# A transformer block on one core: gates brought to all partitions by DMA, VectorE's gating work and the weight rounding moved

## The reference, cut to what matters

```
logits = xt @ gate_w.T                        # 8 experts
scores = softmax(logits); top_scores, sel = top_k(scores, 2)
for e in range(8):                            # tokens routed to e, scaled by their gate
    xe = where(routed to e, xt * gate_e, 0)
    out_routed += (silu(xe @ w1[e]) * (xe @ w3[e])) @ w2[e]
out = out_routed + (silu(xt @ w1s) * (xt @ w3s)) @ w2s    # the shared expert
```

## Time and profile before

| | |
|---|---|
| median of 3 runs | 990.48 us (988.3 to 992.23) |
| profiled execution | 989.17 us, span 987.4 us, mean granted TensorE clock 0.973 |
| busy, share of the span | PE 874.8 us (89%), weight load 621.0 (63%), VectorE 732.5 (74%), ScalarE 578.9 (59%), GpSimd 528.6 (54%) |
| DMA | 8.70 MB in all, mean 9 GB/s; 235 GB/s in the first fortieth of the span |

### The profile page before, as it was taken

How to read it: one execution, slowest core, us unless ns; L and a number is a source line. 1 busy time by engine, 2 the same in 40 slices (tenths; PEclk the granted TensorE clock), 3 DMA queues, 4 the chain that set the end, 5 groups by cost and what they waited for, 6 DMA issues and landing times.

```text
span 987.4 us, 22246 instructions
## 1 busy us (share of the span) xinstructions
PE 874.8 (89%) x7264; PEld 621.0 (63%) x7264; DVE 732.5 (74%) x1978; ACT 578.9 (59%) x903; POOL 528.6 (54%) x610
## 2 busy tenths in 40 slices
PE   2799999888999999999788888888878799999998
PEld 0355555545688777788555555555545688888887
DVE  4677777766777777777678898989883577767775
ACT  1478778766444434444488888888875344444443
POOL 4666666663444455554436575757542644454551
PEclk9999999988999999999899999999997899999999
DMA  8000000000000000000000000000000000000000
GB/s 235 1 2 1 0 0 0 0 2 2 1 1 1 1 1 0 0 1 1 1 2 1 1 0 0 0 0 0 1 1 1 1 12 12 12 7 4 11 11 23
DMA packets 14607, 8.70 MB, mean 9 GB/s; under 512 B 1616, under 2 KB 14160, under 8 KB 14544
## 3 DMA queue, kind: packets, MB, share of 16 engines
q1 hardware_dynamic: 12960, 7.28, 2.6%
q10 hardware_dynamic: 1584, 0.62, 0.2%
HBM read 5.80 MB, written 2.10 MB: 8 GB/s over the span
## 4 chain that ended last, share of the span: by engine, by line
PE 21%; issue 13%; DVE 11%; POOL 7%; ACT 2%; DVEq 0%; POOLq 0%; ACTq 0%
DVE s_qs L1088 6%; PE psum L819 5%; PE psum L787 5%; POOL f_xe_lo L1434 3%; POOL f_p L1444 3%; PE psum L1327 2%; PE psum L769 2%; PE psum L1289 1%; DVE f_xe L1471 1%; PE psum L885 1%; PE psum L1291 1%; PE psum L1290 1%; PE psum L874 1%; PE psum L804 1%; ACT f_xe_hi L1403 1%
## 5 line engine op out<-in xcount | busy, mean ns | idle before, releaser
L1403 ACT ACTIVATE f_xe_hi<-f_xe 128x512 fp32r<-128x512 f32 x128 | 80.9, 632 | 204.6 <-DVE f_xe L1471 204.6
L1434 POOL TENSOR_TENSOR f_xe_lo<-f_xe,f_xe_hi 128x512 fp32r<-128x512 f32 x64 | 83.9, 1311 | 184.6 <-ACT f_xe_hi L1403 184.6
L1088 DVE TENSOR_REDUCE s_qs<-psum 128x4 fp32r<-128x1024 f32 x128 | 156.3, 1222 | 35.4 <-PE psum L804 34.6
L1327 PEld LDWEIGHTS psum<-w,f_h 128*128 128x128 f32 x1152 | 147.7, 191 | 8.8
L1327 PE MATMUL psum<-w,f_h 128*128 128x128 f32 x1152 | 153.0, 276 | 0.0
L467 ACT ACTIVATE s_probs<-psum 128x1024 f32<-128x1024 f32 x128 | 125.9, 1023 | 33.1 <-PE psum L354 32.7
L955 ACT ACTIVATE s_probs<-psum 128x1024 f32<-128x1024 f32 x128 | 131.3, 1026 | 19.5 <-PE psum L787 17.8
L1289 PE MATMUL psum<-f_xe_hi,w_hi 128*128 128x512 f32 x288 | 127.0, 441 | 7.6 <-POOL f_xe_lo L1434 7.0
L1487 DVE TENSOR_TENSOR f_h<-psum,f_g 128x512 f32<-128x512 f32 x144 | 99.2, 689 | 44.9 <-ACT f_g L1388 34.6
L1291 PE MATMUL psum<-f_xe_lo,w_hi 128*128 128x512 f32 x288 | 114.1, 396 | 0.0
L1290 PE MATMUL psum<-f_xe_hi,w_lo 128*128 128x512 f32 x288 | 113.5, 394 | 0.0
(11 more groups left out here) (177 smaller groups left out, 1732.6 us busy)
## 6 DMA issues: line engine op xcount, KB each, us to landing
out<-x SPq DMA_DIRECT2D x8, 256.0 KB, 2.3
x<-in_x SPq DMA_DIRECT2D x3, 512.0 KB, 9.6
w<-in_w SPq DMA_DIRECT2D x3, 512.0 KB, 7.5
x<-in_x SPq DMA_DIRECT2D x2, 256.0 KB, 3.9
select_raw<-in_select SPq DMA_DIRECT2D x1, 512.0 KB, 4.8
rope_cos<-in_rope_cos SPq DMA_DIRECT2D x1, 256.0 KB, 3.9
rope_sin<-in_rope_sin SPq DMA_DIRECT2D x1, 256.0 KB, 4.6
wqkv_a<-in_Wqkv_aT ACTq DMA_DIRECT2D x1, 192.0 KB, 3.6
```

The source lines that it names most:

```text
L1088: dve.tensor_reduce(o[:, r:r + 2, 2 * p:2 * p + 2, 24:25].bitcast(F32R), room(km, i).rearrange("p (r j s) -> p r j s", r=2, j=2), AX.X, AL ...
L1327: ins = pe.matmul(Y[k % 2][:, t * P:(t + 1) * P], g.f_h[:, q, t * P:(t + 1) * P], g.w2[:, e, :], start=(e == 0 and t == 0), stop=(e == NE ...
L1434: pool.tensor_tensor(xe_lo[:, ring(e), :], src, xe_hi[:, ring(e), :], ALU.subtract).then_inc(xe_lo_pool.sem, 1)
```

## The change

- The gates go to all partitions by DMA. VectorE multiplies the chosen gates by the reciprocal sum as before, then turns them in 32x32 blocks (`dve.transpose` into `f_sg`). SyncE's queue writes `f_sg` (16 KB, runs of 128 bytes) to a DRAM tensor `gates`, waits until that has landed, and then loads for each expert one row of 512 gates to all 128 partitions (`f_gt`, 256 KB, a ring of four). For the experts after the first four, and from the second chunk on for all, SyncE waits before each load until VectorE has used the buffer. `scale` now multiplies two SBUF tensors. The selecting matmuls, `s_turn`, `f_st`, `f_ss`, the two instructions that filled it, and the selecting matrices with their load and rounding are gone.
- The norm, transposes, logits, choice and powers of a chunk are done two chunks ahead instead of one, in slots 4 to 8; `best` is cut into `best` and `masks`, `gates` into `sums` and `gates`, `residual` into `residual` and `stats`, each in its own slot. The shared expert's rounding moves from its own turn to slot 2.
- `LOW_ON_DVE` goes from four experts to two; GpSimd's `low` goes from five to seven per chunk.
- `LEAD` starts the feed-forward slots one attention slot earlier in most cases. In attention B two waits for bank 5 and for `f_st` go or come earlier.
- Opening: x is loaded in eight parts, those from the third on only after `first_loads` have landed; ScalarE runs one small exponential before its remaining DMA issues; VectorE's wait for `first_loads` moves from before the first norm to step -2; statistics and roots are spread anew; the Newton rounds of the first two sequences run on VectorE.
- w1 and w3 are rounded in slot 11 of steps 12 and 13, their rests are made in slot 5 of steps 13 and 14.
- The output stores of the second feed-forward layer are issued between the gate loads of chunk m and m+2.

The core of the diff; "..." marks what is left out:

```diff
-PARTS = ((0, 4), (4, 8), (8, 16), (16, 24), (24, 32))
-STATISTICS = ((-3, 0), (-2, 11), (-1, 12), (0, 8), (0, 12))
-ROOTS = ((-3, 0), (-2, 15), (-1, 15), (0, 15), (1, 5))
+PARTS = tuple((t, t + 4) for t in range(0, NT, 4))
+LOADED = ((0, 1), (1, 1), (2, 2), (2, 2), (3, 4), (3, 4), (3, 4), (3, 4))
+STATISTICS = {(-3, 0): (0,), (-3, 11): (1, 2), (-2, 3): (3,), (-2, 12): (4, 5), (-1, 12): (6, 7)}
+ROOTS = {(-3, 0): (0,), (-2, 5): (1, 2, 3), (-1, 5): (4, 5), (0, 5): (6, 7)}
...
-            sp.dma_start(g.x[:, lo:hi, :], x_view[:, lo:hi, :]).then_inc(x_loaded[i], 16)
+            if i == 2:
+                sp.wait_ge(first_loaded, first_count)
+            sp.dma_start(g.x[:, lo:hi, :], x_view[:, lo:hi, :]).then_inc(x_loaded[LOADED[i][0]], 16)
...
+                act.wait_ge(filled, 1)
+                act.activation(tiny[:, 60:61], g.minus_half[:, 0:1], ACT.Exp)
...
+            if (k, h) == (-2, 2):
                 dve.wait_ge(first_loaded, first_count)
...
+NEWTON_ON_DVE = 2
...
-            if k in (13, 14):
-                pool.wait_ge(g.late_loaded, g.late_count)
-                pool.wait_ge(w_hi_sb.sem, k - 12)
-                w, hi, lo = ((g.w1, g.w1_hi, g.w1_lo), (g.w3, g.w3_hi, g.w3_lo))[k - 13]
-                pool.tensor_tensor(lo[:], w[:], hi[:], ALU.subtract)
+                if k in (13, 14) and h == 5:
+                    pool.wait_ge(w_hi_sb.sem, k - 12)
+                    w, hi, lo = ((g.w1, g.w1_hi, g.w1_lo), (g.w3, g.w3_hi, g.w3_lo))[k - 13]
+                    pool.tensor_tensor(lo[:], w[:], hi[:], ALU.subtract)
...
+                if km < NEWTON_ON_DVE:
+                    dve.wait_ge(seed.sem, seed.upto(m))
+                    i = 0
+                    for o, u, w, op in newton_steps():
+                        if i:
+                            dve.wait_ge(newton.sem, newton.upto(m, i))
+                        dve.tensor_tensor(o[:], u[:], w[:], op).then_inc(newton.sem, 1)
...
-            if k == 12:
-                dve.wait_ge(g.late_loaded, g.late_count)
-                dve.tensor_copy(g.w1_hi[:], g.w1[:]).then_inc(w_hi_sb.sem, 1)
-                dve.tensor_copy(g.w3_hi[:], g.w3[:]).then_inc(w_hi_sb.sem, 1)
-                dve.tensor_copy(g.select[:], g.select_raw[:])
             for h in part:
+                if k in (12, 13) and h == 11:
+                    dve.wait_ge(g.late_loaded, g.late_count)
+                    w, hi = ((g.w1, g.w1_hi), (g.w3, g.w3_hi))[k - 12]
+                    dve.tensor_copy(hi[:], w[:]).then_inc(w_hi_sb.sem, 1)
...
-LOW_ON_DVE = (2, 5, 6, 7)
+LOW_ON_DVE = (2, 3)
+LOW_ON_POOL = (0, 1, 4, 5, 8, 6, 7)
 BESIDE = {-3: (0, 0, 0, 1, 1, 1, 2, 2, 2, 2, 3, 3, 3, 4, 4, 4),
           -2: (4, 5, 5, 5, 6, 6, 6, 6, 7, 7, 7, 8, 8, 8, 8, 8)}
-LEAD = {1: (0,), 3: (1,), 4: (2,), 6: (3,), 8: (4,), 9: (5,), 13: (6,), 15: (7,)}
+LEAD = {0: (0,), 2: (1,), 3: (2,), 5: (3,), 6: (4,), 7: (5,), 13: (6,), 15: (7,)}
 TAIL_A = {1: ((-1, 8),), 4: ((0, 0),), 8: ((0, 1),), 11: ((0, 2),), 14: ((0, 3),),
           15: ((0, 4), (0, 5), (0, 6), (0, 7), (0, 8))}
 TAIL_B = {1: ((-1, 8),), 4: ((0, 0),), 8: ((0, 1), (0, 2), (0, 3)), 12: ((0, 4),), 14: ((0, 5),),
           15: ((0, 6), (0, 7), (0, 8))}
 FF = {
-    "norm": 8, "x_turn": 0, "xt_sb": 0, "logits": 1, "best": 1, "pow": (2, 2, 2, 2), "gates": 5, "s_turn": 6,
-    "st_sb": 6, "residual": 0, "rstd": 0,
+    "norm": 4, "x_turn": 5, "xt_sb": 5, "logits": 6, "best": 7, "masks": 8, "pow": 7, "sums": 2, "gates": 3,
+    "residual": 5, "stats": 6, "rstd": 8, "shared": 2,
 }
-FF_LEAD = {"x_turn": 0, "xt_sb": 1, "logits": 2, "best": 2, "exp": 4, "gates": 5, "s_turn": 6, "st_sb": 6}
+FF_LEAD = {"x_turn": 0, "xt_sb": 1, "logits": 2, "best": 2, "masks": 2, "exp": 4, "sums": 5, "gates": 5}
...
+    written, gt_sb = ev("written", 16), [ev(f"gt_sb{i}", 16 * E // 4) for i in range(4)]
...
+    def turned(n, k, e, task):
+        return ([(n + 1, k + 1)] if k == -1 and e == FF_LEAD[task] else []) + (
+            [(n + 2, k + 2)] if k + 2 < NCH and e == FF[task] else [])
...
+    def inputs(n, k, e):
+        return [x for x in ahead(n, k, e, 3) if x[2] < E] + ([(n, k, E)] if e == FF["shared"] and 0 <= k < NCH else [])
...
-            def spread(m, km, e):
-                if e == 0:
-                    if km == 0:
-                        pe.wait_ge(before.turned.sem, before.turned.upto(last))
-                    pe.wait_ge(st_sb.sem, st_sb.upto(m))
-                    pe.wait_ge(xe_sb.sem, xe_sb.upto(m - 1))
-                else:
-                    pe.wait_ge(xe_sb.sem, xe_sb.upto(m, e))
-                pe.matmul(SB, g.select[:, e, :], st[:, km % 2, :],
-                          start=True, stop=True).then_inc(sb_mm.sem, 1)
...
-            def s_turn():
-                pe.wait_ge(lo_sb.sem, lo_sb.upto(n + 1))
-                for t in range(4):
-                    ins = pe.transpose(T[:, t * P:(t + 1) * P], ssp[:, t, :], g.identity[:])
-                ins.then_inc(st_mm.sem, 1)
...
-                if gate and e == AT["st_sb"]:
-                    act.wait_ge(st_mm.sem, st_mm.upto(n + 1))
-                    act.activation(st[:, (k + 1) % 2, :], T, ACT.Copy).then_inc(st_sb.sem, 1)
...
+                if e == FF["pow"] and k + 2 < NCH:
+                    pool.wait_ge(sh_sb.sem, sh_sb.upto(n + 2))
+                    w = 4 * E // PIECES
+                    for i in range(PIECES):
                         pool.tensor_tensor(g.f_p[:, i * w:(i + 1) * w], g.euler[:, 0:w],
                                            g.f_sh[:, i * w:(i + 1) * w], ALU.pow).then_inc(pw_sb.sem, 1)
...
-                dve.wait_ge(sb_mm.sem, sb_mm.upto(m, e + 1))
+                dve.wait_ge(xt_sb.sem, xt_sb.upto(m))
+                dve.wait_ge(gt_sb[e % 4].sem, gt_sb[e % 4].upto(m, 16 * (e // 4 + 1)))
...
-                dve.tensor_tensor(xe[:, e % 2, :], SB, xt[:, km % 2, :], ALU.mult).then_inc(xe_sb.sem, 1)
+                dve.tensor_tensor(xe[:, e % 2, :], gt[:, e % 4, :], xt[:, km % 2, :], ALU.mult).then_inc(xe_sb.sem, 1)
...
-                dve.wait_ge(sc_sb.sem, sc_sb.upto(n + 1))
-                dve.wait_ge(st_mm.sem, st_mm.upto(n))
-                dve.tensor_copy(ssp[:, :, 0:E].bitcast(F32R), g.f_m[:, 0, :, :]).then_inc(hi_sb.sem, 1)
-                dve.wait_ge(hi_sb.sem, hi_sb.upto(n + 1))
-                dve.tensor_tensor(ssp[:, :, E:2 * E], g.f_m[:, 0, :, :], ssp[:, :, 0:E], ALU.subtract).then_inc(lo_sb.sem, 1)
+                dve.wait_ge(sc_sb.sem, sc_sb.upto(m))
+                dve.wait_ge(written.sem, written.upto(m - 1))
+                dve.transpose(g.f_sg[:], g.f_m[:, 0, :, :].rearrange("p t e -> p (t e)")).then_inc(sg_sb.sem, 1)
...
+        def store(m):
+            view = out.rearrange("(n s) (c p) d -> n p (s c) d", s=2, p=P)
+            sp.wait_ge(x_sb.sem, x_sb.upto(Step(None, 0, m)))
+            sp.dma_start(view[m], g.x[:, 4 * m:4 * m + 4, :]).then_inc(stored, 16)
+        for m in range(NCH):
+            n = Step(None, 0, m)
+            sp.wait_ge(sg_sb.sem, sg_sb.upto(n))
+            sp.dma_start(g.gates[m % 2].rearrange("e (t b j) -> b (e t) j", t=4, b=4),
+                         g.f_sg[:]).then_inc(written.sem, 16)
+            sp.wait_ge(written.sem, written.upto(n))
+            for e in range(E):
+                if e >= 4 or m > 0:
+                    sp.wait_ge(xe_sb.sem, xe_sb.upto(n, e - 3) if e >= 4 else xe_sb.upto(n - 1, e + 5))
+                sp.dma_start(gt[:, e % 4, :], g.gates[m % 2, e].partition_broadcast(P)).then_inc(gt_sb[e % 4].sem, 16)
+                if not first and e == 3 and m >= 2:
+                    store(m - 2)
+        if not first:
+            for m in (NCH - 2, NCH - 1):
+                store(m)
+            sp.wait_ge(stored, 16 * NCH)
...
+                for m, km in turned(n, k, e, "best"):
+                    best(m)
+                for m, km in turned(n, k, e, "masks"):
+                    masks(m)
+                for task, by in (("sums", sums), ("gates", gates)):
+                    if k == -1 and e == FF_LEAD[task] or k >= 0 and k + 1 < NCH and e == FF[task]:
+                        by(n + 1)
                 if 0 <= k - 1 < NCH and e == FF["residual"]:
                     residual(n - 1, k - 1)
+                if 0 <= k - 1 < NCH and e == FF["stats"]:
+                    stats(n - 1)
...
```

176 lines of the change are left out of this document (73 added, 103 removed).

## The result

The changed kernel takes 1062.8 us (1061.21 to 1066.12, 4 runs), the one before 990.99 (988.3 to 992.23): ratio 1.0755, 95% interval 1.0726 to 1.0785. It is 7.5% slower; 945 with a range of 908 to 980 had been forecast.

What follows compares the result with a forecast made beforehand. TensorE's own work plus short stalls was taken as the feed-forward bound. From 989.2 us, opening -5, weights -5.5, chunks -9, -20 and -1, edges -5 gave 943.7; with 1.3 for the median, 945, range 908 to 980.

Steps and rivals of the forecast that it cites:

- GpSimd's order: Feed-forward chunks: GpSimd's queue stalls TensorE 2.6 us at expert 4 in the first layer, 0.4 in the second; later about 0.9.
- the floor: Feed-forward chunks: TensorE's work falls from 24.2 to 21.8 us, -5.3 us in the first layer and -4.8 in the second.
- GpSimd's powers ahead of expert 4: Feed-forward chunks: powers delay GpSimd's subtraction for expert 4, stalling TensorE 2.6 us in the first layer, 0.4 in the second.
- Two SBUF inputs: VectorE's gating, now reading SBUF twice, collides with GpSimd's subtractions, not its powers: 2.5 us a chunk.
- The way through DRAM: Feed-forward gates written to DRAM and reloaded: 6.7 us against 6.3 us of cover, 0.5 us of stall per chunk.
- C: Rival, feed-forward: the 256 KB gate loads don't keep up, chunks take 36 us, about 1130 us in all; chance 0.05.
- D: Rival, feed-forward: the gates' way is late by more than 3 us, chunks near 27, 985 to 995 us; chance 0.06.
- VectorE's sum: Feed-forward chunks: VectorE's work is 22.1 us in the first layer, about 20 in the second.
- Weights: Attention A: rearranged weight rounding gives back 5.5 of 7.4 us, bounds -7.4 and 0.
- Opening: Start of the kernel: earlier bias and Newton rounds on VectorE give -5 us, bounds -9 and +2.
- B: Rival: powers hold VectorE too, or GpSimd's queue is later than drawn; chunks 27.1 and 25.5, 977 us; chance 0.18.
- Edges: First chunk of each feed-forward layer and the chunk beside attention B lose 8 selects each: -5 us in all.

Runs made afterwards that it cites:

- experiment 1: Changed kernel with GpSimd's subtraction for each expert waiting for that expert's own rounding, the shared one for the seventh instead of the ninth: 993.73 us, ratio 1.0071.
- experiment 14: Changed kernel with shared subtraction in slot 4, VectorE gating before the hidden product, subtractions of experts 4 and 7 on VectorE, and the old opening: 915.55 us, ratio 0.929.
- Experiment 5: Kernel before the change, with only VectorE's order swapped so the gating comes before the hidden product: 971.7 us, ratio 0.9862.
- experiment 2: Changed kernel with the shared expert's rounding and subtraction back in slot 5, behind experts 6 and 7: 984.71 us, ratio 0.9977.
- experiment 4: The kernel of experiment 2 with VectorE gating the next input before it forms the hidden product: 946.22 us, ratio 0.9589.
- experiments 6 and 7: Subtraction of expert 4 moved from GpSimd to VectorE, on the kernel of experiment 2 (982.68 us), then on that of experiment 4 (930.48 us).
- experiment 10: Kernel before the change, with only the rounding of w1 and w3 and their rests rearranged: 983.08 us, ratio 0.995.
- experiments 11 to 13: On experiment 4 plus expert 4's subtraction on VectorE, shared in slot 4 (930.87 us): old opening 924.74; no SyncE wait 925.22; Newton steps on GpSimd 925.39 us.

## Why the prediction was wrong

**The step that failed first** is in "GpSimd's order": "Further `low` 1.28 us apart (5, the shared one, 6, 7) then stay ahead of 2.29 us slots". I took durations and order of GpSimd's queue, but not what its waits count. The change moved the shared rounding on ScalarE and left `upto(m, e + 1)`, which counts roundings, not experts. The diff doesn't show that line, because it is the same in both kernels; only the order that it counts changed. Instead of 0.9 us per chunk in the first layer it cost 4.4 us there and 4.0 in the second: 69 us with the edges (experiment 1).

**The second** is the floor: "So 2.9 us are stalls in the first feed-forward layer and 2.4 in the second" and "That is the floor of a chunk after". The sum of TensorE's work was right (experiment 14). But the forecast adds its new stalls to 21.8 and carries nothing over of the 2.9 and 2.4 us of old ones, without a reason. Experiment 5 shows that 1.6 and 1.0 us of them came from the order on VectorE, and that stayed: the ring holds an undisturbed slot at 2.59 us, 0.06 above TensorE's 2.53 before. So taking 0.24 us from each of these slots on TensorE frees nearly nothing: chunks of 26.5 and 25.6 in experiment 2 where 25.6 and 23.3 were forecast. No sum of busy times shows a ring; the idle times do, 1.47 us before each rounding and 0.70 before each VectorE subtraction, the same in slot after slot. The order cost 38.5 us (experiment 4).

**What the forecast had as small**: the shared input in slot 2 meets VectorE, 9 us (experiment 2), 0.7 to 0.8 us a chunk; it was forecast as one collision of 1.3 us on VectorE, of which nothing entered the sum of a first-layer chunk.

From 1062.8 these three lead to 946.2, by the chain of experiments 1, 2 and 4. That this is the number forecast is partly luck, since two terms err in opposite senses: the opening was put at -5 and costs +3 to +7, and the chunks are then 24.6 and 23.2 instead of 25.6 and 23.3.

**Point by point.** *GpSimd's powers ahead of expert 4*: right in kind, 1.35 us in a first-layer chunk and 0.65 in the second (experiment 2) where 2.6 and 0.4 stood; taking the subtraction away pays only once the ring is gone (2 against 15.7 us, experiments 6 and 7). *Two SBUF inputs*: right in kind. An `f_xe` beside GpSimd's subtraction takes 1.47 us (362.36) and 0.69 beside powers; means are 731 ns in the changed kernel and 918 in experiment 4, where 682 stood before. That is 0.4 and 1.9 us in eight of a chunk, against 2.5 forecast. *The way through DRAM*: right; 0.5 us a chunk were allowed, 4.9 us in all were measured, and rivals C and D fell with loads of 3.4 us. *VectorE's sum*: right, it never became the bound. *Weights*: right within the attention layer (6.9 us in steps, 5.5 forecast), 3.9 alone over the whole kernel (experiment 10). *Opening*: wrong in sign. The bias did land 2.3 us earlier and the first norm did move by 1.6. But "more x parts to wait for", given as a bound of +2, became a stand of 4 to 5 us with the q, k, v addition behind it, and the Newton steps on VectorE, taken as -2.5, took 3.1 us there instead of 2.4 and delayed the next norm; either alone is harmless (experiments 11 to 13). *Rivals*: by time C (about 1130) and D (985 to 995) stood nearest, each some 68 us off and with a mechanism that VectorE's 4.9 us of waits for the gates refutes. B was nearest in kind, with GpSimd's queue later than drawn; but its chunks of 27.1 and 25.5 are near those of the kernel with the wait mended (27.2 and 26.4), and there VectorE's order sets them. No rival had 31. *Edges* (-5): no run tells them apart.

The Trainium skill, page "SBUF — State Buffer", section "Who interferes with whom", says that a VectorE instruction with two SBUF inputs and a GpSimd one that reads SBUF exclude each other. For subtractions the trace agrees (1.47 us against 0.68). For the powers it shows it from GpSimd's side only: VectorE keeps 0.68 us, but the four powers grow from 6.44 us before to 6.81 in the changed kernel and 7.65 in experiment 4.

## What to carry to other kernels

Where work moves in an order, reread every wait that counts that order: a count is tied to the sequence, not to the item. Before taking work off the busiest engine, follow one turn of the pipeline from an instruction back to itself over all engines; if the sum of starts equals the pace, the ring holds that stretch, and swapping two independent instructions on one engine can be worth more than removing a tenth of TensorE's work (the swap alone -15 us in experiment 5; the removal with the right waits and the old order -2 in experiment 2, whose interval reaches 1.0005). Repeat a small edit that gave nothing once the larger limit is gone.

## What the runs showed of the hardware that had not been expected

A DMA from DRAM to all partitions of 256 KB lands in 3.3 to 3.4 us (median of 128) while the core moves 95 to 105 GB/s (experiment 14); VectorE waited 6.7 us for such loads in all 16 chunks there, 4.9 in the changed kernel. Soon behind a TensorE stall of 4.5 us the matmuls come 0.43 us apart instead of 0.23 (373.78 to 375.06, granted clock 0.50), and by 377.3 it is 1.00 again; so such a stall costs more than its own length. GpSimd's powers take 1637 ns each in the mean before, 1896 in experiment 4 and 1922 in experiment 14, while VectorE's `f_xe` and `f_xe_lo` beside them keep 0.68 to 0.69 us.
